# A wait for landed gathers ahead of each slot's gathers on GpSimd

## The reference

```python
h = jnp.maximum(_layernorm(x, axis=-1), 0.0)
...
xs = x[src]
for i in range(W.shape[0]):
    mask = (edge_types == i)[:, None]
    msgs = msgs + jnp.where(mask, xs @ W[i] + b[i], 0.0)
out = jax.ops.segment_sum(msgs, dst, num_segments=N)
...
x = x + _L0_gnn_ref(h, edge_index, edge_type_4, L0_gnn_W, L0_gnn_b)
```

## Time and profile before

| | before |
|---|---|
| median of 3 runs | 1995.47 us (1995.43 to 1996.4) |
| the profiled execution, span from the first to the last instruction | 2330.0 us |
| profiled execution against the median | 334.5 us longer |
| mean granted TensorE clock in the profiled execution | 0.655 |
| GpSimd busy | 1476.5 us (63%), 1572 instructions |
| TensorE matmul busy | 912.9 us (39%) |
| VectorE busy | 615.1 us (26%) |
| ScalarE busy | 134.3 us (6%) |

### The profile page before, as it was taken

One profiled execution on the slowest core, in us unless ns is written; L12 is line 12 of the kernel. 1 busy time (PEld: TensorE's weight loads), 2 busy tenths in 40 slices (PEclk: granted clock), 3 DMA queues, 4 the chain that ended last, 5 costly groups with the idle time before them and its releaser, 6 DMA issues.

```text
span 2330.0 us, 18844 instructions
## 1 busy us (share of the span) xinstructions
PE 912.9 (39%) x4019; PEld 665.1 (29%) x4020; DVE 615.1 (26%) x1537; ACT 134.3 (6%) x384; POOL 1476.5 (63%) x1572
## 2 busy tenths in 40 slices
PE   5773214333434343444434343334333333323225
PEld 2331213323222322233323232323223232222224
DVE  5555112222221212222222222222222222111115
ACT  3340000000000000000000000000000000000000
POOL 6664666656666666666667566667676666666660
PEclk8886567666666666655666566666666676665557
DMA  8662111111111111111111111111111111511114
GB/s 245 217 213 94 45 49 45 46 36 45 47 45 47 45 47 45 47 45 45 47 43 49 41 45 45 47 43 49 43 49 43 48 44 48 155 45 47 45 47 118
DMA packets 107776, 151.14 MB, mean 65 GB/s; under 512 B 27235, under 2 KB 69937, under 8 KB 107745
## 3 DMA queue, kind: packets, MB, share of 16 engines
q0 software_dynamic: 50016, 102.53, 17.3%
q1 hardware_dynamic: 53335, 45.89, 6.1%
q10 hardware_dynamic: 4394, 2.40, 0.4%
HBM read 118.62 MB, written 32.09 MB: 65 GB/s over the span
## 4 chain that ended last, share of the span: by engine, by line
another core or an unknown queue 29%; issue 23%; DVEq 19%; PE 17%; DVE 10%; DMA 0%; ACT 0%; ACTq 0%; SPq 0%
PE ps_sum L786 6%; PE ps_y L815 5%; PE ps_y L734 4%; DVEq L264 4%; DVEq L637 3%; DVE lists L618 3%; DVEq L618 3%; DVEq L610 2%; DVEq L606 2%; DVEq L641 1%; DVE acc L610 1%; DVEq L636 1%; DVEq L617 1%; DVEq L628 1%
## 5 line engine op out<-in xcount | busy, mean ns | idle before, releaser
L379 POOL DMA_INDIRECT messages<-message_table,table_row x1155 | 1089.7, 943 | 583.5 <-issue 339.8
L786 PE MATMUL ps_sum<-lists,messages 128*128 128x128 f32 x1776 | 310.8, 350 | 576.9 <-DVE acc L610 463.6
L786 PEld LDWEIGHTS ps_sum<-lists,messages 128*128 128x128 f32 x1776 | 294.3, 260 | 591.0 <-issue 591.0
L379 POOL DMA_INDIRECT lists<-message_table,table_row x288 | 271.6, 943 | 157.7 <-issue 84.1
L610 DVE TENSOR_TENSOR acc<-acc,ps_sum x200 | 56.8, 284 | 899.6 <-remote 776.0
L786 PE MATMUL ps_sum<-onehot,messages 128*128 128x128 f32 x582 | 111.8, 370 | 408.2 <-DVE acc L610 271.1
L618 DVE SCALAR_TENSOR_TENSOR lists<-ps_node,lists,dst_col 128x512 f32<-128x512 f32 x296 | 212.9, 748 | 156.9 <-issue 117.4
L786 PEld LDWEIGHTS ps_sum<-onehot,messages 128*128 128x128 f32 x582 | 104.0, 277 | 414.7 <-issue 414.7
L815 PE MATMUL ps_y<-stage 128*128 128x512 f32 x136 | 106.2, 825 | 128.9 <-issue 95.2
L366 POOL DMA_INDIRECT early_x<-in_x,src_col x120 | 113.6, 947 | 65.6 <-issue 33.8
L641 DVE TENSOR_TENSOR lists<-lists,tile_base 128x1 f32 x200 | 32.8, 164 | 435.4 <-issue 429.9
(11 more groups left out here) (87 smaller groups left out, 503.6 us busy)
## 6 DMA issues: line engine op xcount, KB each, us to landing
message_table<-stage SPq DMA_DIRECT2D x98, 256.0 KB
messages<-message_table,table_row POOLq DMA_INDIRECT x1155
early_x<-in_x SPq DMA_DIRECT2D x6, 896.0 KB
out<-acc SPq DMA_DIRECT2D x6, 896.0 KB
lists<-message_table,table_row POOLq DMA_INDIRECT x288
acc<-in_x SPq DMA_DIRECT2D x4, 896.0 KB
early_x<-in_x,src_col POOLq DMA_INDIRECT x120
acc<-in_x ACTq DMA_DIRECT2D x2, 896.0 KB, 5.7
```

What stands on the lines that cost most here:

```text
L379: pool.indirect_dma_start(messages[k][:, t, :], None, table_rows, bass.IndirectOffsetOnAxis(ap=flat_rows[:, at + t:at + t + 1], axis=0)).t ...
L786: ins = nc.tensor.matmul(ps_sum[:, bass.ds(q % BANKS, 1), 0:d], messages[k][:, t, :], onehots[k][:, t, :], start=(t == 0), stop=(t == tile ...
```

## The change

Ahead of the gathers of slot k of round i GpSimd waits until all 8 gathers of the slot before it in the order (slot k - 1 of the same round, for k = 0 slot 4 of the round before) have landed. The counts waited for are constants. The wait applies to 180 of the 181 slots: for the first one there is nothing to wait for, and `wait` leaves out a value of zero. Nothing else is changed.

```diff
             def gather(i, k, tiles=SB_TILES):
+                before = (i, k - 1) if k else (i - 1, SLOTS - 1)
+                wait(pool, gathered[before[1]], (before[0] + 1) * (16 * SB_TILES))
                 pool.wait_ge(slot_free[k], i + 1)
                 at = (EARLY_SBS + i * SLOTS + k) * SB_TILES
                 for t in range(tiles):
```

## The result

| | before | after |
|---|---|---|
| median of the timed runs, one chip | 1995.6 us (1995.43 to 1996.4) | 2277.7 us (2276.4 to 2279.3) |
| ratio, 95% interval | | 1.1412 [1.1398, 1.1426] |
| profiled execution, span | 2330.0 us | 2277.5 us |
| idle before L379 / L381 (`messages` + `lists`) | 741.2 us | 724.9 us |

The change made the kernel 282 us slower. That is above the range on record (2150 to 2275) and 56 us above the forecast of 2222.

A forecast was written before the change was run, and what follows sets the result against it. GpSimd was taken to bound the kernel, issuing gathers without waits in a run. The runs' 1995.5 us plus 222 us for 180 boundaries plus 5 us for the reload of `x` made 2222 us, range 2150 to 2275.

The forecast's parts named there:

- GpSimd sets the pace at 1.248 us a gather, and a run has no waits for slots: GpSimd's table gathers: issued 1.248 us apart in runs; the profile's 278 us of waits for TensorE's freeing are absent there.
- slowness of the profiled execution: TensorE's and VectorE's stops around GpSimd's pauses: said to belong to the profiled execution, not to the runs' work.
- The landing, "I take 2.20": Last gather of a slot: lands 2.20 us after its start, read from when the DMA engines stop being busy.
- The estimate by the Trainium skill: Landing of a 64 KB gather: about 2.0 us fixed plus bytes over 436 GB/s, 2.15 us, giving 213 us in all.
- The range: Whole kernel's time: 2166 to 2253 us for the forecast itself, widened to 2150 to 2275 us.
- GpSimd's restart, 0.28 us: GpSimd at a boundary: next gather starts 0.28 us after the awaited landing, with ends of 0.15 and 0.45 us.
- 180 boundaries: Between slots on GpSimd: every one of 180 boundaries pays 1.23 us, 222 us together, with nothing hiding it.
- The reload of x, 5 us: Boundaries while SyncE's queue loads `x` again: two of them cost 2.5 us more each, 5 us together.
- A dearer boundary: Slot boundaries: restart dearer or landing nearer 2.69 us, so 310 us more and 2305 us in all; chance 7%.
- The waits on slots are real: GpSimd's waits for free slots occur in runs and pay for the new waits: about 2000 us, not slower; chance 6%.
- the pauses help: Silences after each slot let TensorE and VectorE go on: 278 us vanish, 264 us are paid, 1981 us; chance 3%.
- the span may change little: Profiled execution of the changed kernel: new pauses of 222 us replace 278 us of old waits, though runs get slower.

The follow-up runs named there:

- two_slots_back: The changed kernel with each slot's wait set on the slot two back, not the one before: 1995.7 us, ratio 0.9998 to the kernel before, on the faster chip.
- experiment 3: The changed kernel with the wait ahead of slot 0 alone, once a round, 36 times: 2049.4 us, ratio 1.0268 to the kernel before, on the faster chip.
- 2 and 4: The changed kernel with the wait ahead of each slot's third gather, 2000.9 us; and with the wait for the slot two back, 1995.7 us; kernel before 1995.6 us.
- change_again: The changed kernel, unaltered, timed and profiled on a slower chip beside the kernel before: 2323.6 us against 2326.6, ratio 0.9976.
- experiment 9: Changed kernel on slower chips, ratios to the kernel before: wait at slot 0 alone 1.0296, ahead of each second gather 1.0100, for the slot two back 1.0184.

## Why the prediction was wrong

*GpSimd sets the pace at 1.248 us a gather, and a run has no waits for slots:* right for the chip that was timed, as the profile of `two_slots_back` shows. The arithmetic behind it (1995.5 us leave no room for waits) was sound, the reason given for the difference was wrong. The prediction said of TensorE's and VectorE's stops that they are "slowness of the profiled execution"; they are slowness of the chip from which that profile came, and runs on such chips have them too (2326 to 2340 us on five chips). That the base was right all the same is in part luck: had the change been timed on a slower chip, it would have made no difference (2326.6 and 2323.6 us).

*The landing, "I take 2.20":* this is the step that failed. The sum took the last DMA packet for the landing, and the semaphore's last update comes 0.3 us later, at 2.5 us. 0.32 x 180 = 58 us, and with 4 us less for the restart and 2 more for the reload that is the whole error of 56. A nearer figure was at hand in the earlier trace rows, where TensorE starts 2.69 us after the slot's last gather. In the profile after, TensorE starts 2.66 us after it and GpSimd 0.09 us behind TensorE (1011.25 and 1011.34), so TensorE's own start adds little to the landing. The estimate by the Trainium skill ("DMA: Bandwidth & Descriptors", anatomy of one DMA on the gpsimd path) was 2.15 us, and the trace puts 2.5 in its place.

*The range:* the sum's own ends were 171 and 288 us, and the 276 us that the boundaries cost lie between them. The range was cut at 252 us (1.40 us a boundary) and widened to 2275 only, without a reason for leaving out the upper end; with 288 it would have reached 2288.

*GpSimd's restart, 0.28 us:* right, 0.26 us; in this program the gather itself holds the wait that ends last. With the order turned round it is 0.76 us, on slower chips.

*180 boundaries:* right; a fifth of them cost a fifth (experiment 3), and a wait that is met costs nothing on this chip (2 and 4). *The reload of x, 5 us:* two boundaries of 6.43 and 6.07 us in place of 2.78, so 7 us.

With these the sum is 180 x (2.52 + 0.26 - 1.248) + 7 = 283 us; measured were 282.

*The rivals.* "A dearer boundary" (7%) named the failing term, at 2305 us. "The waits on slots are real" did not hold on the faster chip; on the slower ones the outcome was the one that it gives, no difference, and there the mechanism is that of "the pauses help": with a stop at every slot VectorE's slow sequencer instructions all but vanish (533 to 35), and some 274 us of waits fall away while 286 us of pauses are paid. The prediction also said that in a profiled execution like the one of before the span may change little for this reason, and that is what `change_again` shows.

*What stays open:* what makes a chip slower. In the stretch of the gathers it is VectorE's sequencer that is slow while gather follows gather; why it is so on these chips alone isn't shown. In the first stretch, where no table gather runs, a slower chip is 47 us behind as well, and there at most two of these instructions are slow, so that is something else. Short or rare pauses (experiment 9) have no sum that fits. The step at every eleventh slot has no cause shown. No experiment took the gathers away from beside the matmuls.

## What to carry to other kernels

To wait for the landing of a small gather before issuing the next costs, per wait, the landing at the semaphore plus the restart less the turn at which the queue would have been anyway: here 2.52 + 0.26 - 1.25 us. Put the wait two gathers later, or on an older transfer, and it was free on the faster chip. Where one instruction has two waits, put the one that ends last first in the program, so that the gather itself holds it (0.26 us against 0.76); a second wait that is always met can still move the first one and make it dearer. Take the landing from the first instruction that starts on it, and not from the last packet. And before a span and a median that differ by a sixth are explained by profiling, ask whether they come from the same chip: the same edit was worth 14% on one and nothing on another.

## What had not been expected

- The same program takes 1995.6 us on one chip and 2326 to 2340 us on five others.
- From the last DMA packet of a gather to the semaphore's full count some 0.3 us go by (2.2 and 2.5 us after the start).
- The order of two waits ahead of a gather moved the time by 109 us (180 boundaries) on a slower chip: 0.76 us from the landing to the gather when an instruction of its own holds the wait, 0.26 us when the gather itself does.
- A met wait per slot cost nothing on the faster chip (0.9998) and 45 us on a slower one, most of it since it put the wait for the free slot into an instruction of its own.
- On a slower chip 533 of VectorE's some 3300 sequencer instructions took over 0.4 us beside an unbroken stream of gathers, 35 with a pause at every slot; on the faster chip none did.
